# One output projection for two attention blocks, in place of one per block, in an 8-core transformer layer

## The reference, cut to what matters

```python
# x: (4, 4096, 1024) float32, 16 heads of 64
x = x + 0.5 * ffn(layernorm(x))
x = x + attn(layernorm(x))
x = x + 0.5 * ffn(layernorm(x))

def ffn(x):                       # x_prev is x one token earlier
    xr = mu_r * x + (1 - mu_r) * x_prev
    xk = mu_k * x + (1 - mu_k) * x_prev
    return sigmoid(xr @ W_r) * (square(relu(xk @ W_k)) @ W_v)

def attn(x):                      # chunks of 10 tokens, 25 tokens of left context
    q, k, v = (proj(x, W, b) for each of the three)
    probs = softmax(q * 64**-0.5 @ k.T + mask)
    return (probs @ v) @ Wo.T + bo
```

## Time and profile before

| | us |
|---|---|
| median of two runs | 4460.92 |
| the two runs | 4433.60 and 4488.24 |
| the profiled execution's own time | 4437.68 |
| span of its slowest core (core 6) | 4436.2 |
| spans of the eight cores | 4400.0 to 4436.2 |
| mean granted TensorE clock, by core | 0.752 to 0.759 of full speed |

### The profile page before, as it was taken

How to read it: one execution, slowest core, us unless ns; L and a number is a source line. 1 busy time by engine, 2 the same in 40 slices (tenths; PEclk the granted TensorE clock), 3 DMA queues, 4 the chain that set the end, 5 groups by cost and what they waited for, 6 DMA issues and landing times.

```text
span 4436.2 us, 70660 instructions; the slowest of 8 cores (4400.0 to 4436.2 us)
## 1 busy us (share of the span) xinstructions
PE 3451.5 (78%) x27248; PEld 2318.9 (52%) x27248; DVE 1431.4 (32%) x2777; ACT 871.2 (20%) x1809; POOL 347.3 (8%) x572
## 2 busy tenths in 40 slices
PE   0037899996677899997687789998767698999677
PEld 0025555654555654655465555565555465565456
DVE  3413323334232223334313232333333232333431
ACT  2322211112223111112222121111122211111221
POOL 2311000001111000000101000000111100000110
PEclk6568986666888896756787798566688899665679
DMA  7651110002021211000212010100202110100021
GB/s 232 206 192 39 77 39 40 3 1 77 39 73 46 103 50 40 2 2 1 77 58 98 39 77 39 41 2 1 77 39 106 51 77 39 40 2 2 1 77 58
DMA packets 48763, 250.61 MB, mean 56 GB/s; under 512 B 12593, under 2 KB 28977, under 8 KB 43314
## 3 DMA queue, kind: packets, MB, share of 16 engines
q0 software_dynamic: 14720, 197.14, 11.4%
q1 hardware_dynamic: 33714, 48.96, 3.9%
HBM read 208.33 MB, written 37.75 MB: 55 GB/s over the span
## 4 chain that ended last, share of the span: by engine, by line
PE 67%; DMA 11%; DVE 11%; ACT 5%; issue 5%; POOL 1%; DVEq 0%; ACTq 0%; SPq 0%; POOLq 0%
PE gp L539 21%; PE sb L539 12%; PE sb L684 7%; PE pv L778 6%; PE misc L745 5%; PE sb L681 3%; PE misc L419 2%; DMA wsl<-sc_wfv 2%; PE sb L618 2%; PE gp L618 2%; DMA wsl<-sc_wfr 2%; PE misc L452 2%; DVE bfBl L443 2%; DMA y<-X 2%; ACT bfBh L441 2%
## 5 line engine op out<-in xcount | busy, mean ns | idle before, releaser
L539 PE MATMUL gp<-bfAh,wsl 128*128 128x280 bf16 x2048 | 395.8, 296 | 217.4 <-DMA wsl<-sc_wfr 141.5
L539 PE MATMUL gp<-bfAl,wsl 128*128 128x280 bf16 (+2 forms) x2048 | 545.1, 277 | 0.0
L539 PE MATMUL sb<-bfAh,wsl 128*128 128x280 bf16 x2048 | 394.5, 295 | 99.0 <-DMA wsl<-sc_wfv 52.7
L539 PE MATMUL sb<-bfAl,wsl 128*128 128x280 bf16 x1280 | 373.1, 291 | 0.0
L539 PEld LDWEIGHTS gp<-bfAh,wsl 128*128 128x128 bf16 x2048 | 206.8, 102 | 279.3 <-issue 226.7
L539 PE MATMUL gp<-T,wsl 128*128 128x256 bf16 (+2 forms) x2048 | 305.2, 263 | 11.5 <-DMA wsl<-sc_wq 8.3
L693 ACT ACTIVATE e<-sb,nb,sc 128x384 f32<-128x384 f32 (+1 forms) x160 | 100.4, 628 | 1054.7 <-PE sb L688 1054.7
L681 PE MATMUL sb<-msb,idt 128*128 128x128 bf16 x832 | 230.2, 277 | 92.9 <-DVE qbl L653 62.3
L539 PEld LDWEIGHTS sb<-bfAh,wsl 128*128 128x128 bf16 x2048 | 206.4, 102 | 160.0 <-issue 107.5
L700 DVE TENSOR_TENSOR el<-e 128x384 bf16<-128x384 f32 (+1 forms) x160 | 80.8, 505 | 601.5 <-ACT e L695 601.5
L539 PE MATMUL gp<-bfBh,wsl 128*128 128x280 bf16 x1024 | 197.6, 295 | 59.4 <-ACT katmp L565 59.4
(11 more groups left out here) (176 smaller groups left out, 6445.8 us busy)
## 6 DMA issues: line engine op xcount, KB each, us to landing
wsl<-sc_wfr POOLq DMA_DIRECT2D x8, 4096.0 KB, 15.9
wsl<-sc_wfk POOLq DMA_DIRECT2D x8, 4096.0 KB, 18.9
wsl<-sc_wfv POOLq DMA_DIRECT2D x8, 4096.0 KB, 12.5
wsl<-sc_wak POOLq DMA_DIRECT2D x4, 4096.0 KB, 12.6
wsl<-sc_wav POOLq DMA_DIRECT2D x4, 4096.0 KB, 13.8
wsl<-sc_wq POOLq DMA_DIRECT2D x4, 4096.0 KB, 12.4
wsl<-sc_wo POOLq DMA_DIRECT2D x4, 4096.0 KB, 13.3
X<-x SPq DMA_DIRECT2D x8, 1120.0 KB, 5.8
```

Of the source, the lines that this page charges most:

```text
L539: ins = t.matmul(out_ap, wap(slot, reg, ci, d0, dn), rhs, start=first, stop=(ci == NCH - 1 and j == 2))
```

## The change

`attn_wo` now projects two blocks at once, 256 columns wide, so there are three per pass (b0 with b1, b2 with b3, b4 alone) instead of five. For this `am32` is replaced by `aeh` and `ael` with room for two blocks, one small float32 buffer `pvt` takes the product by the reciprocals, ScalarE rounds it to the high part `aeh`, and VectorE, no longer GpSimd, subtracts to get `ael`. `preempt` is gone: Wo of b0 and b1 stands behind the pairs of b1, Wo of b2 and b3 behind those of b3. The pairs of b3 therefore stand ahead of the weave with the LayerNorm, no longer in it.

```diff
-    am32 = A("am32", [128, NCH * 128], F32)
-    ael = A("ael", [128, NCH * 128], BF16)
+    aeh = A("aeh", [128, NCH * 256], BF16)
+    ael = A("ael", [128, NCH * 256], BF16)
...
+    pvt = A("pvt", [128, 128], F32)
...
-    def attn_wo(q, bi, oslot, osres, passlbl):
+    def attn_wo(q, bi0, nb2, oslot, osres, passlbl):
...
-                return emit_mm24(t, gp[_g][:, 0:_sz], _oslot, _dj * 128, 128,
-                                 lambda ci: amv()[:, ci * 128:ci * 128 + _sz],
-                                 lambda ci: ael[:, ci * 128:ci * 128 + _sz])
+                return emit_mm24(t, gp[_g][:, 0:_n], _oslot, _dj * 128, 128,
+                                 lambda ci: aeh[:, ci * 256:ci * 256 + _n],
+                                 lambda ci: ael[:, ci * 256:ci * 256 + _n])
...
-        st("vector", lambda v, _pr=pr, _sz=sz, _bk=bk_i:
-           v.tensor_tensor(out=am32[:, _pr * 128:_pr * 128 + _sz], in0=pv[_bk][:, 0:_sz],
-                           in1=rb32[:, 0:_sz], op=ALU.mult),
-           r=["pv%d" % bk_i, "rb32"], w=["aeh"], note=lbl + " pvm p%d" % pr)
-        st("gpsimd", lambda g, _pr=pr, _sz=sz:
-           g.tensor_tensor(out=ael[:, _pr * 128:_pr * 128 + _sz],
...
-           r=["aeh"], w=["ael"], note=lbl + " al p%d" % pr)
+        st("vector", lambda v, _sz=sz, _bk=bk_i:
+           v.tensor_tensor(out=pvt[:, 0:_sz], in0=pv[_bk][:, 0:_sz], in1=rb32[:, 0:_sz], op=ALU.mult),
+           r=["pv%d" % bk_i, "rb32"], w=["pvt"], note=lbl + " pvm p%d" % pr)
+        po = pr * 256 + (bi % 2) * 128
+        st("scalar", lambda s, _po=po, _sz=sz: s.copy(out=aeh[:, _po:_po + _sz],
+                                                      in_=pvt[:, 0:_sz]),
+           r=["pvt"], w=["aeh%d" % (bi % 2)], note=lbl + " ah p%d" % pr)
+        st("vector", lambda v, _po=po, _sz=sz:
+           v.tensor_tensor(out=ael[:, _po:_po + _sz], in0=pvt[:, 0:_sz],
+                           in1=aeh[:, _po:_po + _sz], op=ALU.subtract),
+           r=["pvt", "aeh%d" % (bi % 2)], w=["ael%d" % (bi % 2)], note=lbl + " al p%d" % pr)
...
-            attn_pairs(q, 1, 128, qslot, qsres, at,
-                       preempt=lambda: attn_wo(q, 0, oslot, osres, at))
+            attn_pairs(q, 1, 128, qslot, qsres, at)
+            attn_wo(q, 0, 2, oslot, osres, at)
             attn_Q_pair(qslot, qsres, 2, 2, at)
-            attn_pairs(q, 2, 0, qslot, qsres, at,
-                       preempt=lambda: attn_wo(q, 1, oslot, osres, at))
+            attn_pairs(q, 2, 0, qslot, qsres, at)
+            attn_pairs(q, 3, 128, qslot, qsres, at)
...
-            attn_wo(q, 2, oslot, osres, at)
-            bgb = (groups_of(attn_pairs, q, 3, 128, qslot, qsres, at)
-                   + groups_of(attn_Q_pair, qslot, qsres, 4, 1, at)
-                   + groups_of(attn_pairs, q, 4, 0, qslot, qsres, at,
-                               preempt=lambda: attn_wo(q, 3, oslot, osres, at))
-                   + groups_of(attn_wo, q, 4, oslot, osres, at))
+            attn_wo(q, 2, 2, oslot, osres, at)
+            bgb = (groups_of(attn_Q_pair, qslot, qsres, 4, 1, at)
+                   + groups_of(attn_pairs, q, 4, 0, qslot, qsres, at)
+                   + groups_of(attn_wo, q, 4, 1, oslot, osres, at))
             weave(capture(cm_ln3), bgb, lead=12)
```

More of the change, by code:

```diff
@@ L232, in thi_sview @@
         return T.ap().bitcast(BF16).rearrange("p (c t two) -> p c t two", c=NCH, two=2)[:, :, a:b, 1]
-    def amv():
-        return am32.ap().bitcast(BF16).rearrange("p (n two) -> p n two", two=2)[:, :, 1]
     def ehv(pb):
@@ L656, in attn_Q_pair, with attn_pairs @@
                r=["gp%d" % g, "battn", "qbh"], w=["qbl"], note=lbl + " ql%d" % dj)
-    def attn_pairs(q, bi, qoff, qslot, qsres, passlbl, preempt=None):
+    def attn_pairs(q, bi, qoff, qslot, qsres, passlbl):
         lbl = "%s.b%d" % (passlbl, bi)
@@ L709, in attn_pairs @@
                 tail_a(pr - 1, lbl, sz, ws, pieces)
-            if pr == 2 and preempt is not None:
-                preempt()
             if pr > 1:
-                tail_b(pr - 2, lbl, sz, ws, pieces)
+                tail_b(pr - 2, lbl, sz, ws, pieces, bi)
         tail_a(NCH - 1, lbl, sz, ws, pieces)
-        tail_b(NCH - 2, lbl, sz, ws, pieces)
-        tail_b(NCH - 1, lbl, sz, ws, pieces)
-    def attn_wo(q, bi, oslot, osres, passlbl):
-        lbl = "%s.b%d" % (passlbl, bi)
-        r0, sz = BLOCKS[bi]
+        tail_b(NCH - 2, lbl, sz, ws, pieces, bi)
@@ L721, in attn_wo @@
+        tail_b(NCH - 1, lbl, sz, ws, pieces, bi)
+    def attn_wo(q, bi0, nb2, oslot, osres, passlbl):
+        lbl = "%s.b%d+%d" % (passlbl, bi0, nb2)
+        r0 = BLOCKS[bi0][0]
+        n = sum(BLOCKS[bi0 + j][1] for j in range(nb2))
+        ares = ["aeh%d" % ((bi0 + j) % 2) for j in range(nb2)]
+        ares += ["ael%d" % ((bi0 + j) % 2) for j in range(nb2)]
         for dj in range(NCH):
             g = dj % 2
-            def mm(t, _dj=dj, _g=g, _sz=sz, _oslot=oslot):
-                return emit_mm24(t, gp[_g][:, 0:_sz], _oslot, _dj * 128, 128,
-                                 lambda ci: amv()[:, ci * 128:ci * 128 + _sz],
-                                 lambda ci: ael[:, ci * 128:ci * 128 + _sz])
@@ L727, in attn_wo, with mm @@
[L727 to L731, removed]
+            def mm(t, _dj=dj, _g=g, _n=n, _oslot=oslot):
+                return emit_mm24(t, gp[_g][:, 0:_n], _oslot, _dj * 128, 128,
+                                 lambda ci: aeh[:, ci * 256:ci * 256 + _n],
+                                 lambda ci: ael[:, ci * 256:ci * 256 + _n])
@@ L732, in attn_wo @@
+            st("tensor", mm, r=ares + osres, w=["gp%d" % g], note=lbl + " Wo%d" % dj)
+            st("vector", lambda v, _dj=dj, _g=g, _r0=r0, _n=n:
+               v.scalar_tensor_tensor(out=X[:, _dj * P + _r0:_dj * P + _r0 + _n],
+                                      in0=gp[_g][:, 0:_n], scalar=bos[:, _dj:_dj + 1],
+                                      in1=X[:, _dj * P + _r0:_dj * P + _r0 + _n],
                                       op0=ALU.add, op1=ALU.add),
-               r=["gp%d" % g, "battn"], w=hres("X", r0, r0 + sz), note=lbl + " Woev%d" % dj)
+               r=["gp%d" % g, "battn"], w=hres("X", r0, r0 + n), note=lbl + " Woev%d" % dj)
@@ L756, in tail_a, with tail_b @@
         st("vector", rsev, r=["misc"], w=["rs32_%d" % (pr % 2)], note=lbl + " rs p%d" % pr)
-    def tail_b(pr, lbl, sz, ws, pieces):
+    def tail_b(pr, lbl, sz, ws, pieces, bi):
         pb = pr % 3
@@ L868, in build_nc @@
                                 attn_pairs(q, bi0 + j, 128 * j, qslot, qsres, at)
-                                attn_wo(q, bi0 + j, oslot, osres, at)
+                            attn_wo(q, bi0, nb2, oslot, osres, at)
             ysth(q, 0)
```

2 lines of the change are left out of this document (removed).

## The result

The changed kernel took 4466.0 us (median of 11, 4459.6 to 4689.7). Some executions of any of these kernels take longer, with a lower clock on half or all of the chip, and the ratios leave them out, so a median can lie above what its ratio says. The profiled execution took 4464.28 us against 4437.68 before, +26.6; I had forecast +8.

A forecast was written before the change was run, and what follows sets the result against it. TensorE was taken to set the time, except from Q4 to f2, where the LayerNorm chain and `wfr` load decide. Terms summed to +2.4 us a pass, +9.8 in four; with -3.7 and +2, 4437.7 + 8 = 4446 us, range 4405 to 4488.

The forecast's parts named there:

- waits in front of them: Waits for `ael` ahead of the two wide Wo: one more hand-over, 3.0 us a pass in place of 1.1, +1.9.
- the mean: LayerNorm's mean, before in the pairs of b3, leaves them: -6.05 us a pass there.
- Q4: Stretch from Q4 to b4's first scores: 8.5 us in place of 21.0, -12.5 us a pass.
- Rival 2: A wide matmul is cheaper than two narrow ones: 20.5 in place of 23.8 us per block, 4420 us; chance 0.05.
- Rival 4: The clock stays low in warm blocks too: each wide Wo and Q 41 us, 4660 us in all; chance 0.02.
- Rival 1: The section's end overlaps as before: b4 about 75 us in place of 89, 4390 us in all; chance 0.14.
- Rival 3: b4 covers nothing of the LayerNorm chain: section 101 us, 12 more a pass, 4494 us in all; chance 0.17.
- LayerNorm and the pairs of b4: From b4's first scores to f2: chain with 65 background groups, not 122; 89.0 us against 74.1, +14.9 a pass.
- Ten more steps and the broadcast, 8.0: In b4's section, ten TensorE steps at 0.72 us each and the mean's broadcast: 8.0 us.
- ten steps and the second broadcast, 8.1: In b4's section after the variance, ten TensorE steps and the second broadcast: 8.1 us.
- With nothing beside it a 4 MB load took 12.42.: Basis for pricing the `wfr` load, issued at once after GpSimd's last mix: last VectorE mix to f2 14.4 us.
- -3.7 in three: In q0 to q2 the old load took up to 16.83 us, not 15.37; a load alone gives that back.

The follow-up runs named there:

- experiments 1 and 2: Changed kernel with each two-block Wo made as two 128-wide calls at the same place; ratios to the kernel before 1.0024, then 1.0031.
- 9: Changed kernel with both the finer LayerNorm weave and each two-block Wo as two 128-wide calls; lowest 4381.39 us, no interval.
- experiment 8: Changed kernel with only the weave order around f2's LayerNorm replaced, groups spread finely; 0.9894 of the kernel before, median 4387.82 us.
- experiments 11 and 12: Kernel before with the ScalarE and VectorE path and a finer weave, nothing merged; first lowest 4364.34 us, then ratio 0.983, median 4365.66 us.
- Experiment 6: Changed kernel with f2's `wfk` load held until TensorE has done one group of r; ratio to the kernel before 1.0058.

## Why the prediction was partly wrong

**Right.** The sign against the profiled execution, the class (within 2%) and the range 4405 to 4488 held. Step by step: wide Wo 23.8 and 23.3 us cold and Q 21.7 warm (forecast 23.8, 23.8, 21.7); waits in front of them 2.8 us a pass (3.0), by experiments 1 and 2 and again 9; the pairs of b0 to b3 without these waits +8.3 (forecast +9.3 for b1 to b3, +0.5 for b0), by longer matmuls and not by waits; the mean 6.03; Q4 -12.4 (-12.5). Rival 2 fell: 192 wide matmuls at the upper clock took 21.66 us, 112.8 ns each, and 192 narrow ones 10.88 us, 56.7 ns each (the second calls of experiments 1 and 2). The Trainium skill ("TensorE: Matmul & The Clock Gate", section "Back-to-back issue gap") would have a wide one cost less than two narrow ones; the traces disagree here too. Rival 4 fell: the upper clock came in every wide Wo, 2.6 to 6.0 us after its start. Rival 1 fell as a forecast for this order, but experiment 8 shows that its mechanism was there to be had by another order. Rival 3 had the right place and mechanism (TensorE through with its groups, waiting for the chain) and the wrong size: b4's section came to 93.0, not 101.

**Wrong: the sum of 89.0 us for "LayerNorm and the pairs of b4".** It measured 93.0. Its two terms of ten steps and its term for the load were too small, and the others hold to 0.3 us:
- "Ten more steps and the broadcast, 8.0" and "ten steps and the second broadcast, 8.1" took 9.1 and 9.0. I had priced ten steps at TensorE's mean of 0.72 us. The rows of VectorE and TensorE above show what I left out: the low parts of the exponentials, the reciprocals and `rb` of b4's tails stand on VectorE in order, `rb` comes at 4197.80, and TensorE waits 2.46 us for it with the broadcast, which alone takes 1.27. Between two steps of the chain stands not only TensorE's work but a round through ScalarE and VectorE that nothing covers.
- "With nothing beside it a 4 MB load took 12.42." That was `wq`. From VectorE's last mix to f2 I had 1.6 + 0.3 + 12.5 = 14.4; measured 1.69 - 0.06 + 14.57 = 16.2. With it falls the "-3.7 in three": the load took nearly as long as before (14.86 then), and it was not alone, since the neighbour's stood beside it. It is the place and not the tensor: ahead of f1 in pass q3 the same `wfr` landed after 12.6 to 12.8 us on cores 1, 2, 4 and 6 of the changed kernel.

Together +4.0 a pass, and 0.8 more because 74.1 was pass q3 on one core, and the mean section before was 73.3. 4 x 4.8 = 19 us, which is the gap between +8 and +26.6; the other differences (dense blocks and pairs 1.7 a pass better than forecast, Q of b0 and b1 0.4 worse, the 3.7 that fell) about cancel. That they do is luck. I took one pass of one core for the base and a load at another place for the price; both errors pointed the same way.

**What was missed besides.** I set the number against the profiled execution, and 4446 lies under the median shown (4460.9), while the kernel in fact got slower. A change of +8 was also a small remainder of terms up to 15 us a pass, so that 4 us in one of them made it three times as large. And I counted the change as one move. It is three, which the experiments part: the new path gains 6.4 us a pass, merging b0 with b1 loses 4.4, emptying the weave of b3 loses 8.5. My terms for the first (the load issued 7 us sooner, the longer hand-over) stood inside the b4 sum and the waits and were never summed up by themselves; had I done that, the path alone would have been in sight as a version of its own. And the wait of 12.4 us at Q4, which I gave to merging, goes without it (experiments 11 and 12).

**Still open.** Why in the changed kernel `wfr` for f2 never lands under 13.4 us, even on the core that issues first, where other loads and `wfr` itself ahead of f1 come in 12.6; in experiment 8 it landed in 12.5 to 12.8 us on five cores in the last pass. Experiment 6 removes a part of its spread, not its floor.

## What to carry to other kernels

A filler is worth what it covers at the moment, not its sum: when work is taken out of a mix of a latency chain with a background, price every wait of the chain again, with what is left between it and the next; and before giving the filler up, try to spread what is left (here 16.4 us a pass). Making one wide step of two narrow ones saves nothing where loads were hidden, and makes its start wait for the younger input. Take a base from all cores and passes, not from one.

## What the runs showed of the hardware

- Weight loads under 128-column matmuls were hidden: two narrow calls with 384 loads took 23.55 us, one wide with 192 loads 23.78 and 23.28. At the upper clock a narrow matmul with its load took 56.7 ns and a wide one 112.8.
- The wide Wo of b0 and b1 behind pairs was granted the upper clock after 5.5 us in the mean (2.6 to 6.0), that of b2 and b3 after 4.5 (3.8 to 5.6), two narrow calls at the same places after 4.0 and 4.1. On core 5 in q3 it came after 2.6 us (0.76 in the mean of the first 5.52 us), and that block took 22.4 us. In length the means of wide and narrow differ by 0.3 us at most. I had taken the start from Wo of b0 before (2.7 us).
- In the pairs behind Q on core 5 TensorE was busy for 139.52 of 146.57 us, and the granted clock was 0.50 all the while.
- A 4 MB load of `wfr` took 13.6 to 16.9 us from its issue to f2's first matmul in the changed kernel. The 4 MB loads of `wfv` and `wq` landed after 12.3 to 14.4 us there, with medians of 12.6 and 12.7. In all four passes, but for one case of sixteen, the slower load of `wfr` was on cores 0, 3, 5 and 7, one of each two neighbours: the one that issued later (experiment 6).
